# The causal mask as a matrix product, and every fourth low-part subtraction on GpSimd, in a fused decoder block

## The chip, the cores and the metric

One core of a Trainium2 chip runs the whole block in one launch. The metric is the device time of the kernel in microseconds (us); the time of a kernel is the median of its runs. TensorE multiplies matrices, VectorE and ScalarE work elementwise, GpSimd elementwise too and issues the indirect transfers, and SyncE issues most of the others.

## What is computed

Two batches of 1024 tokens of width 256 go through a decoder block in float32: causal self-attention with 16 query heads of 64 and one shared key and value head, cross-attention to 77 context rows, and a feed-forward layer with four experts of which each token takes one. The part that matters here, cut from the reference:

```python
q, k = (l2norm(q), l2norm(k))
q, k = (q * srt, k * srt)            # srt = 4
sim = jnp.einsum('bhid,bjd->bhij', q, k)
causal_mask = jnp.triu(jnp.ones((n, n), dtype=bool), 1)
sim = jnp.where(causal_mask, max_neg, sim)
attn = jax.nn.softmax(sim.astype(jnp.float32), axis=-1)
out = jnp.einsum('bhij,bjd->bhid', attn, v)
```

Since queries and keys have length one before scaling, no score exceeds 16 and the exponentials need no maximum; the row sum comes from a column of ones beside the values.

## The kernel before

**Tiles and steps.** The 2048 tokens are 16 tiles of 128 rows, eight for each batch. The self-attention is a list of 288 steps (t, g, j): tile t, group g of four heads, key tile j from 0 to t mod 8. One step makes a block of scores S, 128 keys by 4 x 128 queries (512 columns), and adds its share to the output O. Tile t has 4 x (t mod 8 + 1) steps; this stretch is called slot t here, and its steps are counted from 0. The last step of each group lies on the diagonal (`on_diagonal`): there keys later than the query must be taken out. There are 64 such steps.

**Precision.** Products in the fast format `F32R` keep fewer bits, so operands are split into a high and a low part. A step takes two products for the scores (L1097, L1098: high and low part of the keys in one tile) and three for the output: values high with `ph` (L1113), values low with `ph` (L1114), values high with `pl` (L1116). `ph` is the exponential rounded to `F32R`, `pr` the exact one, and `pl = pr - ph`.

**Who does what in a step.** TensorE writes S. Off the diagonal ScalarE writes `ph` (L635) and `pr` (L637), and VectorE subtracts (L849). On the diagonal ScalarE writes `pr` only, GpSimd sets the masked part of `pr` to zero (L550), VectorE copies it to `ph` (L847) and then subtracts. `pr`, `ph` and `pl` are rings of four (`RING`); the scores of step k + 3 are issued right after the output products of step k (`AHEAD` = 3).

**Side work.** Between the steps lies all other work of nearby tiles: normalisation, query projection, transposes, output projection, cross-attention, router. `plan_side` spreads it by hand-given positions (`STAGES`), and each engine walks through the same list in `program(engine)`: at position n it does step n and then the side work of position n - `LATER[engine]`. Each engine runs its list in order. GpSimd's side work is mainly powers of -0.5: `roots` of one column (L543), and once per tile the 17 inverse lengths `rn` (L560, stage `qkv_sums`), which waits for VectorE's row sums (L873) and their clamped form `ssc` (L878). After the head outputs are transposed, VectorE scales them (`heads_out`, L900 and L904). Stage `out_proj` ends in a root on GpSimd too.

**After the steps** the tokens are routed, scattered by expert and sent through the experts; the change doesn't touch that.

Of the kernel before, what the change touches and what calls it, by code (L numbers as in the profile page):

```python
# [30 lines left out]
TPB = SEQ // P  # L31
# [3 lines left out]
HPG = HEADS // GROUPS  # L35
# [13 lines left out]
SIM_SCALE = 16.0  # L49
RING = 4  # L50
# [45 lines left out]
AHEAD = 3  # L96


LATER = {"pe": 0, "dve": 2, "act": 3, "pool": 3}
# [85 lines left out]
def build(nc, x, wqkv_t, wout_t, g1, g2, ctx_t, xwq_t, xwk_t, xwv_t, xwout_t, biases, xbout,  # L185
          wr_t, w_v, w_proj, out):
    steps, group_start = plan_steps()
    N_STEPS = len(steps)
# [9 lines left out]
    with ExitStack() as keep:  # L198
        def sem(name):
            return keep.enter_context(nc.semaphore(name))  # L200

        def sb(ctx, name, shape, dt=F32):
            return ctx.enter_context(nc.sbuf_tensor(name, shape, dt))
# [12 lines left out]
        half = sb(keep, "half", [P, HEADS + 2])  # L216
        logits = sb(keep, "logits", [P, TILES, EXP])
# [143 lines left out]
        masked = sem("masked")  # L361
        ph_by_act = sem("ph_by_act")
        ph_by_dve = sem("ph_by_dve")
        pl_ready = sem("pl_ready")
# [71 lines left out]
        def on_diagonal(k):  # L436

            return steps[k][2] == steps[k][0] % TPB

        diagonals = list(itertools.accumulate(int(on_diagonal(k)) for k in range(N_STEPS)))  # L440

        def ph_wait(eng, k):

            if on_diagonal(k):
                eng.wait_ge(ph_by_dve, diagonals[k])
            else:
                eng.wait_ge(ph_by_act, k + 1 - diagonals[k])
# [11 lines left out]
        def _(sp):  # L459
# [19 lines left out]
            sp.wait_ge(consts, 10)  # L479
# [22 lines left out]
        def _(pool):  # L502

            nc.gpsimd.memset(ident[:], 0.0).then_inc(consts, 1)
            nc.gpsimd.memset(tri[:], 1.0).then_inc(consts, 1)
            nc.gpsimd.memset(own[:], 1.0).then_inc(consts, 1)
# [3 lines left out]
            pool.wait_ge(consts, 6)  # L510
# [4 lines left out]
                                    pattern=[[1, P]], channel_multiplier=-1).then_inc(consts, 1)  # L515

# [11 lines left out]
            pool.wait_ge(consts, 10)  # L528
# [16 lines left out]
            for k, stages in program("pool"):  # L545
                if k is not None and steps[k][2] == steps[k][0] % TPB:

                    pool.wait_ge(p_ready, k + 1)
                    blk = pr[:, k % RING, :].rearrange("p (h q) -> p h q", h=HPG)
                    nc.gpsimd.affine_select(out=blk, in_=blk, compare_op=ALU.is_ge, fill=0.0, base=0,  # L550
                                            pattern=[[0, HPG], [1, P]], channel_multiplier=-1).then_inc(masked, 1)
# [59 lines left out]
        def _(act):  # L611
# [14 lines left out]
            for n, (k, stages) in enumerate(program("act")):  # L626
                if k is not None:

                    act.wait_ge(s_ready, k + 1)
                    if k >= RING:  # L630
                        act.wait_ge(pl_ready, k - RING + 1)
                    if not on_diagonal(k):
                        if k >= RING:
                            act.wait_ge(pv_done, k - RING + 1)
                        nc.scalar.activation(ph[:, k % RING, :], S[k % AHEAD][:], ACT.Exp, scale=SIM_SCALE)\  # L635
                            .then_inc(ph_by_act, 1)
                    nc.scalar.activation(pr[:, k % RING, :], S[k % AHEAD][:], ACT.Exp, scale=SIM_SCALE)\  # L637
                        .then_inc(p_ready, 1)
# [122 lines left out]
        def _(dve):  # L761
# [67 lines left out]

            dve.wait_ge(w_in, 32)  # L830
# [3 lines left out]
            diag = 0  # L834
            for k, stages in program("dve"):
                if k is not None:
                    t, _, j = steps[k]

                    if j == t % TPB:
                        diag += 1  # L840
                        dve.wait_ge(masked, diag)
                    else:
                        dve.wait_ge(p_ready, k + 1)
                    if k >= RING:
                        dve.wait_ge(pv_done, k - RING + 1)
                    if on_diagonal(k):
                        nc.vector.tensor_copy(ph[:, k % RING, :], pr[:, k % RING, :]).then_inc(ph_by_dve, 1)  # L847
                    ph_wait(dve, k)
                    nc.vector.tensor_tensor(pl[:, k % RING, :], pr[:, k % RING, :], ph[:, k % RING, :].bitcast(F32),  # L849
                                            ALU.subtract).then_inc(pl_ready, 1)  # L850
# [234 lines left out]
        def _(pe):  # L1085
            pe.wait_ge(consts, 10)
# [12 lines left out]

            def values_of(k):  # L1100
# [256 lines left out]
```

## Time and profile before

| | us |
|---|---|
| median of 3 runs | 1081.1 (1076.33 to 1081.51) |
| the profiled execution, its own time | 1082.78 |
| its span in the profile | 1081.0 |
| TensorE busy | 902.4 |
| VectorE busy | 619.5 |
| ScalarE busy | 545.8 |
| GpSimd busy | 236.9 |

The mean granted clock of TensorE was 0.932 of full speed. Matrix products overlap in the pipeline, so the duration shown for one (about 0.39 us at 512 columns) is longer than the distance between two starts. PE is TensorE, PEld its weight loads, DVE VectorE, ACT ScalarE, POOL GpSimd, SP SyncE.

### The profile page before, as it was taken

The page shows a single profiled execution, that of the slowest core. Times are in us where ns is not written, and L with a number is a line of the kernel's source. Part 1 is how long each engine was busy: PE and PEld are TensorE (multiplying, and loading weights), DVE is VectorE, ACT ScalarE, POOL GpSimd, SP SyncE. Part 2 cuts the span into 40 slices and gives each one's busy share as a digit, 9 for nine tenths or more (in the row PEclk, how much of TensorE's full clock was granted, in tenths as well). Part 3 has the DMA queues.
Part 4 walks back from the last instruction along what each step waited for, and adds up shares of the span by engine and source line. Part 5 has one row for each costly group of instructions (what it writes and reads, how often), then busy time and mean ns, then how long its engine had stood idle before and what let it go on. Part 6 is the DMA issues. An engine that isn't in the chain of part 4 may idle for free.

```text
span 1081.0 us, 14277 instructions
## 1 busy us (share of the span) xinstructions
PE 902.4 (83%) x4446; PEld 672.9 (62%) x4446; DVE 619.5 (57%) x1383; ACT 545.8 (50%) x1032; POOL 236.9 (22%) x282
## 2 busy tenths in 40 slices
PE   3588998989898998969989898999871099999997
PEld 2466676667575765756757575766550077878775
DVE  3456777766666667657676666667576222222221
ACT  1356657566767664455666757676342122222221
POOL 3223322212112122222222222102102501111111
PEclk9688999999999999889999999999975599999999
DMA  8200000000000000000000000000344400000000
GB/s 274 53 1 1 1 2 1 1 1 1 1 1 1 1 1 1 1 1 1 1 1 1 1 1 1 1 1 1 117 139 164 144 11 20 27 21 29 20 25 4
DMA packets 19175, 29.02 MB, mean 27 GB/s; under 512 B 2079, under 2 KB 15648, under 8 KB 19104
## 3 DMA queue, kind: packets, MB, share of 16 engines
q1 hardware_dynamic: 17008, 22.73, 6.9%
q0 software_dynamic: 1680, 4.21, 1.1%
q10 hardware_dynamic: 416, 1.18, 0.3%
q8 instruction: 39, 0.64, 0.2%
q14 instruction: 32, 0.26, 0.1%
HBM read 21.41 MB, written 7.10 MB: 26 GB/s over the span
## 4 chain that ended last, share of the span: by engine, by line
PE 40%; DVE 6%; issue 3%; POOL 3%; ACT 3%; DMA 1%; DVEq 0%; ACTq 0%; POOLq 0%
PE W L1299 7%; PE S L1276 5%; PE O L1276 5%; PE O L1116 2%; PE W L1187 2%; PE S L1097 2%; PE S L1098 2%; PE O L1113 2%; PE O L1114 2%; PE W L1229 2%; POOL sorted_rows L596 2%; PE W L1209 1%; PE W L1155 1%; ACT hT L744 1%; DVE junk L969 1%
## 5 line engine op out<-in xcount | busy, mean ns | idle before, releaser
L849 DVE TENSOR_TENSOR pl<-pr,ph 128x512 fp32r<-128x512 f32 x288 | 199.2, 704 | 48.9 <-ACT pr L637 35.2
L635 ACT ACTIVATE ph<-S 128x512 fp32r<-128x512 f32 x224 | 135.0, 603 | 135.1 <-PE S L1098 133.0
L637 ACT ACTIVATE pr<-S 128x512 f32<-128x512 f32 x288 | 172.3, 600 | 27.9 <-PE S L1098 27.1
L1113 PE MATMUL O<-ph,vhi 128*65 128x512 f32 x288 | 140.8, 489 | 23.7 <-DVE ph L847 23.7
L1116 PE MATMUL O<-pl,vhi 128*65 128x512 f32 x288 | 117.8, 409 | 23.5 <-DVE pl L849 23.1
L1097 PE MATMUL S<-qT,kT 128*128 128x512 f32 x288 | 116.3, 404 | 0.0
L1114 PE MATMUL O<-ph,vlo 128*65 128x512 f32 x288 | 115.6, 401 | 0.0
L1098 PE MATMUL S<-qT,kT 128*128 128x512 f32 x288 | 115.4, 401 | 0.0
L543 POOL TENSOR_TENSOR rs<-ri,half 128x1 f32<-128x1 f32 x48 | 38.9, 811 | 233.5 <-DVE ri L782 233.4
L1116 PEld LDWEIGHTS O<-pl,vhi 128*65 128x65 f32 x288 | 39.9, 138 | 65.5 <-DVE pl L849 40.9
L752 ACT ACTIVATE gate<-S 128x512 f32<-128x512 f32 x38 | 20.7, 596 | 117.7 <-PE S L1276 117.7
L550 POOL TENSOR_SCALAR_AFFINE_SELECT pr<-pr 128x512 f32<-128x512 f32 x64 | 42.6, 666 | 162.9 <-ACT pr L637 162.8
L1299 PE MATMUL W<-wps,hT 128*128 x304 | 70.6, 385 | 8.1 <-ACT hT L744 8.1
L560 POOL TENSOR_TENSOR rn<-ssc,half 128x17 f32<-128x17 f32 x16 | 54.2, 3388 | 102.8 <-DVE ssc L878 102.8
L1155 PE MATMUL W<-wqkv,zT 128*128 128x384 f32 x192 | 72.3, 508 | 0.6 <-ACT zT L647 0.6
L1097 PEld LDWEIGHTS S<-qT,kT 128*128 128x128 f32 x288 | 55.9, 194 | 24.3 <-issue 1.4
L1299 PEld LDWEIGHTS W<-wps,hT 128*128 128x128 f32 x304 | 56.2, 190 | 19.4 <-issue 12.5
L1113 PEld LDWEIGHTS O<-ph,vhi 128*65 128x65 f32 x288 | 40.3, 140 | 39.0 <-DVE ph L847 21.7
L1098 PEld LDWEIGHTS S<-qT,kT 128*128 128x128 f32 x288 | 55.7, 193 | 13.3
L1187 PE MATMUL W<-wout,onT 128*128 128x256 f32 x256 | 60.4, 390 | 1.0 <-DVE xo L950 1.0
L1276 PE MATMUL S<-whl,fzh 128*128 x152 | 56.0, 430 | 2.7 <-DVE fzl L1056 2.7
L425 POOL DMA_INDIRECT out<-res,xs x19 | 19.6, 1031 | 171.8 <-DVE res L1064 171.8
(170 smaller groups left out, 1683.0 us busy)
## 6 DMA issues: line engine op xcount, KB each, us to landing
raw<-in_w_v SPq DMA_DIRECT2D x16, 512.0 KB, 6.3
wps<-in_w_proj SPq DMA_DIRECT2D x4, 1024.0 KB, 8.8
sorted_rows<-pad_row SPq DMA_DIRECT2D x19, 128.5 KB, 4.2
xs<-sorted_rows SPq DMA_DIRECT2D x19, 128.5 KB, 2.0
wqkv<-in_wqkv_t ACTq DMA_DIRECT2D x1, 1152.0 KB, 6.3
wout<-in_wout_t SPq DMA_DIRECT2D x1, 1024.0 KB, 10.0
xall<-in_x SPq DMA_DIRECT2D x1, 1024.0 KB, 10.7
xall<-in_x SPq DMA_DIRECT2D x1, 768.0 KB, 8.0
```

Source lines behind the costliest of these rows:

```text
L635: nc.scalar.activation(ph[:, k % RING, :], S[k % AHEAD][:], ACT.Exp, scale=SIM_SCALE)\
L637: nc.scalar.activation(pr[:, k % RING, :], S[k % AHEAD][:], ACT.Exp, scale=SIM_SCALE)\
L849: nc.vector.tensor_tensor(pl[:, k % RING, :], pr[:, k % RING, :], ph[:, k % RING, :].bitcast(F32), ALU.subtract).then_inc(pl_ready, 1)
L1097: nc.tensor.matmul(S[k % AHEAD][:], kT[:, ks, 0, :], q, start=True, stop=False)
L1098: nc.tensor.matmul(S[k % AHEAD][:], kT[:, ks, 1, :], q, start=False, stop=True).then_inc(s_ready, 1)
L1113: nc.tensor.matmul(o, vhi[:, vs, 0:DH + 1], ph[:, k % RING, :], start=j == 0, stop=False)
L1114: nc.tensor.matmul(o, vlo[:, vs, 0:DH + 1], ph[:, k % RING, :], start=False, stop=False)
L1116: nc.tensor.matmul(o, vhi[:, vs, 0:DH + 1], pl[:, k % RING, :], start=False, stop=last).then_inc(pv_done, 1)
L1155: mm = nc.tensor.matmul(W[job % WB][:, 0:QB], zT[:, c, :], wqkv[:, c, part * QB:(part + 1) * QB], start=c == 0, stop=c == CH - 1)
L1187: mm = nc.tensor.matmul(W[job % WB][:, 0:DIM], onT[:, c, :], wout[:, c, :], start=c == 0, stop=c == 7)
L1276: mm = nc.tensor.matmul(banks[q][:], rows[:, c, :], flat[:, bass.ds(at, 512)], start=m == 0, stop=m == len(passes) - 1)
L1299: mm = nc.tensor.matmul(W[1][:, 0:DIM], hT[:, c, :], flat[:, bass.ds(at, DIM)], start=c == 0, stop=c == HID // P - 1)
```

## The change

The masked positions get -64 added to their score by a product of the identity with a constant block `below` (-64 where the key is later than the query, else 0), accumulated in the same bank ahead of the two score products; with the scale of 16 the exponential of such a score is zero. So ScalarE writes `ph` and `pr` in every step, and GpSimd's select and VectorE's copy are gone. The subtraction of steps k with k mod 4 = 3 runs on GpSimd, the other 216 stay on VectorE. GpSimd's side work comes two positions late in place of three. The setup gets one memset and one select more on GpSimd and two copies on VectorE.

```diff
+MASKED = -64.0
-LATER = {"pe": 0, "dve": 2, "act": 3, "pool": 3}
+LATER = {"pe": 0, "dve": 2, "act": 3, "pool": 2}
...
+        def low_by_pool(k):
+            return k % 4 == 3
+        def low_wait(eng, k):
+            if low_by_pool(k):
+                eng.wait_ge(pl_by_pool, (k + 1) // 4)
             else:
+                eng.wait_ge(pl_by_dve, k + 1 - (k + 1) // 4)
+        def low_part(engine, eng, done, k):
+            eng.wait_ge(p_ready, k + 1)
+            eng.wait_ge(ph_ready, k + 1)
+            if k >= RING:
+                eng.wait_ge(pv_done, k - RING + 1)
+            engine.tensor_tensor(pl[:, k % RING, :], pr[:, k % RING, :], ph[:, k % RING, :].bitcast(F32),
+                                 ALU.subtract).then_inc(done, 1)
...
+            nc.gpsimd.memset(below[:], MASKED).then_inc(consts, 1)
+            nc.gpsimd.affine_select(out=below[:], in_=below[:], compare_op=ALU.is_gt, fill=0.0, base=0,
+                                    pattern=[[-1, P]], channel_multiplier=1).then_inc(consts, 1)
...
             for k, stages in program("pool"):
-                if k is not None and steps[k][2] == steps[k][0] % TPB:
-                    pool.wait_ge(p_ready, k + 1)
-                    blk = pr[:, k % RING, :].rearrange("p (h q) -> p h q", h=HPG)
-                    nc.gpsimd.affine_select(out=blk, in_=blk, compare_op=ALU.is_ge, fill=0.0, base=0,
-                                            pattern=[[0, HPG], [1, P]], channel_multiplier=-1).then_inc(masked, 1)
+                if k is not None and low_by_pool(k):
+                    low_part(nc.gpsimd, pool, pl_by_pool, k)
...
                     act.wait_ge(s_ready, k + 1)
                     if k >= RING:
-                        act.wait_ge(pl_ready, k - RING + 1)
-                    if not on_diagonal(k):
-                        if k >= RING:
-                            act.wait_ge(pv_done, k - RING + 1)
-                        nc.scalar.activation(ph[:, k % RING, :], S[k % AHEAD][:], ACT.Exp, scale=SIM_SCALE)\
-                            .then_inc(ph_by_act, 1)
+                        low_wait(act, k - RING)
+                    if k >= RING:
+                        act.wait_ge(pv_done, k - RING + 1)
+                    nc.scalar.activation(ph[:, k % RING, :], S[k % AHEAD][:], ACT.Exp, scale=SIM_SCALE).then_inc(ph_ready, 1)
                     nc.scalar.activation(pr[:, k % RING, :], S[k % AHEAD][:], ACT.Exp, scale=SIM_SCALE)\
                         .then_inc(p_ready, 1)
...
+            nc.vector.tensor_copy(below_r[:], below[:]).then_inc(mask_ready, 1)
+            nc.vector.tensor_copy(ident_r[:], ident[:]).then_inc(mask_ready, 1)
...
-                    if on_diagonal(k):
-                        nc.vector.tensor_copy(ph[:, k % RING, :], pr[:, k % RING, :]).then_inc(ph_by_dve, 1)
-                    ph_wait(dve, k)
-                    nc.vector.tensor_tensor(pl[:, k % RING, :], pr[:, k % RING, :], ph[:, k % RING, :].bitcast(F32),
-                                            ALU.subtract).then_inc(pl_ready, 1)
+                    if not low_by_pool(k):
+                        low_part(nc.vector, dve, pl_by_dve, k)
...
-                nc.tensor.matmul(S[k % AHEAD][:], kT[:, ks, 0, :], q, start=True, stop=False)
+                if on_diagonal(k):
+                    if k == 0:
+                        pe.wait_ge(mask_ready, 2)
+                    nc.tensor.matmul(S[k % AHEAD][:], ident_r[:], below_r[:].unsqueeze(1).broadcast_to([P, HPG, P]),
+                                     start=True, stop=False)
+                nc.tensor.matmul(S[k % AHEAD][:], kT[:, ks, 0, :], q, start=not on_diagonal(k), stop=False)
                 nc.tensor.matmul(S[k % AHEAD][:], kT[:, ks, 1, :], q, start=False, stop=True).then_inc(s_ready, 1)
...
-                ph_wait(pe, k)
+                pe.wait_ge(ph_ready, k + 1)
...
-                pe.wait_ge(pl_ready, k + 1)
+                low_wait(pe, k)
                 nc.tensor.matmul(o, vhi[:, vs, 0:DH + 1], pl[:, k % RING, :], start=False, stop=last).then_inc(pv_done, 1)
```

## Rows read from the trace of the kernel before

**Rows 1.** The page's first part: busy time of each engine.

```profile
PE 902.4 (83%) x4446; PEld 672.9 (62%) x4446; DVE 619.5 (57%) x1383; ACT 545.8 (50%) x1032; POOL 236.9 (22%) x282
```

**Rows 2.** Stretches: busy us and instructions, granted clock, DMA share, GB/s.

```profile
46.00:768.00 722.00, 645.69 (x3252) 465.86 (x3252) 492.65 (x1058) 458.11 (x878) 167.40 (x196) 0.96 0.00 1
470.60:480.70 10.10, 5.00 (x20) 3.83 (x19) 5.02 (x9) 2.91 (x6) 4.08 (x2) 0.50 0.01 2
```

**Rows 3.** Waits of TensorE, 46 to 768 us: total, times, longest.

```profile
PE O L1113 <- DVE ph L847: 23.7, 12, 6.8
PE O L1116 <- DVE pl L849: 23.1, 19, 3.3
...
PE W L1179 <- DVE on L904: 4.9, 2, 3.8
```

**Rows 4.** Timeline, end of slot 12: start, duration, instruction, idle before.

```profile
602.35 3.48 POOL L560 TENSOR_TENSOR rn<-ssc,half 128x17 f32<-128x17 f32 x1 [7.36 <-DVE ssc L878]
...
607.78 0.63 PE L1116 MATMUL O<-pl,vhi 128*65 128x512 f32 x1
```

**Rows 5.** Timeline, start of slot 10.

```profile
471.61 3.48 POOL L560 TENSOR_TENSOR rn<-ssc,half 128x17 f32<-128x17 f32 x1 [8.44 <-DVE ssc L878]
...
477.00 0.42 DVE L904 TENSOR_TENSOR on<-W,rl 128x256 f32<-128x256 f32 x1
...
477.57 0.66 PE L1217 MATMUL W<-ident,sc 128*128 128x128 f32 x2 [5.10 <-DVE on L904]
```

**Rows 6.** Timeline of a dense stretch of slot 14.

```profile
684.51 0.59 ACT L637 ACTIVATE pr<-S 128x512 f32<-128x512 f32 x1
...
687.03 0.39 PE L1116 MATMUL O<-pl,vhi 128*65 128x512 f32 x1
...
687.26 0.39 PE L1097 MATMUL S<-qT,kT 128*128 128x512 f32 x1
```

**Rows 7.** Groups of instructions: busy us, mean ns; idle before, by whom.

```profile
L849 DVE TENSOR_TENSOR pl<-pr,ph 128x512 fp32r<-128x512 f32 x288 | 199.2, 704 | 48.9 <-ACT pr L637 35.2 <-PE O L1116 8.5 <-DVE logits L969 1.5
...
L635 ACT ACTIVATE ph<-S 128x512 fp32r<-128x512 f32 x224 | 135.0, 603 | 135.1 <-PE S L1098 133.0
...
L550 POOL TENSOR_SCALAR_AFFINE_SELECT pr<-pr 128x512 f32<-128x512 f32 x64 | 42.6, 666 | 162.9 <-ACT pr L637 162.8
...
L847 DVE CAST ph<-pr 128x512 fp32r<-128x512 f32 x64 | 27.7, 432 | 49.1 <-POOL pr L550 48.2 <-PE O L1116 0.7 <-DVE logits L969 0.2
```

**Rows 8.** Single lines on GpSimd: shortest, median, longest ns.

```profile
L576 POOL TENSOR_TENSOR xa<-xa,g2b x16: 724/736/1056, 82.7 to 781.2; 128x256 f32<-128x256 f32 x16
...
L569 POOL CAST vhi<-qhl x16: 237/238/240, 29.3 to 674.8; 128x64 fp32r<-128x64 f32 x16
```

**Rows 9.** Timeline, end of slot 7.

```profile
392.83 3.48 POOL L560 TENSOR_TENSOR rn<-ssc,half 128x17 f32<-128x17 f32 x1 [6.92 <-DVE ssc L878]
...
393.42 0.44 PE L1116 MATMUL O<-pl,vhi 128*65 128x512 f32 x1 [1.28 <-DVE pl L849]
```

**Rows 10.** Timeline, end of slot 3.

```profile
173.46 3.19 POOL L560 TENSOR_TENSOR rn<-ssc,half 128x17 f32<-128x17 f32 x1 [3.33 <-DVE ssc L878]
...
174.68 0.63 PE L1116 MATMUL O<-pl,vhi 128*65 128x512 f32 x1
```

**Rows 11.** Timeline, two products that waited or ran behind a late `pl`.

```profile
512.70 0.45 PE L1116 MATMUL O<-pl,vhi 128*65 128x512 f32 x1
...
708.60 0.45 PE L1116 MATMUL O<-pl,vhi 128*65 128x512 f32 x1 [1.58 <-DVE pl L849]
```

**Rows 12.** Timeline, slot 7: GpSimd's root and a later product.

```profile
361.21 0.96 POOL L543 TENSOR_TENSOR rs<-ri,half 128x1 f32<-128x1 f32 x1 [8.59 <-DVE ri L782]
...
362.63 0.40 PE L1116 MATMUL O<-pl,vhi 128*65 128x512 f32 x1
```

**Rows 13.** Timeline, slot 6: GpSimd and VectorE at once.

```profile
310.26 0.73 POOL L578 TENSOR_TENSOR xall<-xall,xa 128x256 f32<-128x256 f32 x1
310.34 1.20 DVE L849 TENSOR_TENSOR pl<-pr,ph 128x512 fp32r<-128x512 f32 x1
```

More of the change, by code:

```diff
@@ L216, in build @@
         half = sb(keep, "half", [P, HEADS + 2])
+        below = sb(keep, "below", [P, P])
+        below_r = sb(keep, "below_r", [P, P], F32R)
+        ident_r = sb(keep, "ident_r", [P, P], F32R)
         logits = sb(keep, "logits", [P, TILES, EXP])
@@ L360, in build @@
         p_ready = sem("p_ready")
[L361 to L364, printed above, removed]
+        mask_ready = sem("mask_ready")
+        ph_ready = sem("ph_ready")
+        pl_by_pool = sem("pl_by_pool")
+        pl_by_dve = sem("pl_by_dve")
         pv_done = sem("pv_done")
@@ L438, in on_diagonal @@
             return steps[k][2] == steps[k][0] % TPB
-        diagonals = list(itertools.accumulate(int(on_diagonal(k)) for k in range(N_STEPS)))
-        def ph_wait(eng, k):
-            if on_diagonal(k):
-                eng.wait_ge(ph_by_dve, diagonals[k])
-            else:
-                eng.wait_ge(ph_by_act, k + 1 - diagonals[k])
+        def low_by_pool(k):
[3 more added lines that the diff above has]
+                eng.wait_ge(pl_by_pool, (k + 1) // 4)
+            else:
+                eng.wait_ge(pl_by_dve, k + 1 - (k + 1) // 4)
[6 more added lines that the diff above has]
+                                 ALU.subtract).then_inc(done, 1)
         def freed_count(name, part, t):
@@ L477, in _ @@
             sp.wait_ge(x_in[2], 16)
-            sp.wait_ge(consts, 10)
+            sp.wait_ge(consts, 12)
             for n in range(SORTED):
@@ L509, in _ @@
             nc.gpsimd.memset(pad_row[:], 0.0).then_inc(consts, 1)
-            pool.wait_ge(consts, 6)
+            pool.wait_ge(consts, 7)
             nc.gpsimd.affine_select(out=ident[:], in_=ident[:], compare_op=ALU.not_equal, fill=1.0, base=0,
@@ L526, in _ @@
                            channel_multiplier=0).then_inc(consts, 1)
-            pool.wait_ge(consts, 10)
+            pool.wait_ge(consts, 12)
             def roots_of_x(n):
@@ L828, in _ @@
             nc.vector.memset(vlo[:, :, DH:DH + 2].bitcast(F32), 0.0).then_inc(dconst, 1)
+            dve.wait_ge(consts, 12)
+            nc.vector.tensor_copy(below_r[:], below[:]).then_inc(mask_ready, 1)
+            nc.vector.tensor_copy(ident_r[:], ident[:]).then_inc(mask_ready, 1)
             dve.wait_ge(w_in, 32)
@@ L832, in _ @@
                 nc.vector.tensor_scalar(wqkv[:, c, :], wqkv[:, c, :], g1c[:, c:c + 1], None, ALU.mult).then_inc(wq_scaled, 1)
-            diag = 0
             for k, stages in program("dve"):
                 if k is not None:
[L837 to L846, printed above, removed]
-                        nc.vector.tensor_copy(ph[:, k % RING, :], pr[:, k % RING, :]).then_inc(ph_by_dve, 1)
-                    ph_wait(dve, k)
-                    nc.vector.tensor_tensor(pl[:, k % RING, :], pr[:, k % RING, :], ph[:, k % RING, :].bitcast(F32),
-                                            ALU.subtract).then_inc(pl_ready, 1)
+                    if not low_by_pool(k):
+                        low_part(nc.vector, dve, pl_by_dve, k)
                 for name, part, t, job in stages:
@@ L1085, in _ @@
         def _(pe):
-            pe.wait_ge(consts, 10)
+            pe.wait_ge(consts, 12)
             def scores_of(k):
```

## The prediction

> **What bounds the kernel now.** I read the page first. TensorE is busy for 902.4 us of the span of 1081.0 (83%); VectorE follows with 57% [rows 1]. The table of stretches then shows where the change lives. The 288 steps of the causal attention run from 46 to 768 us. There TensorE is busy for 645.7 of 722 us at a granted clock of 0.96, VectorE for 492.7, ScalarE for 458.1 and GpSimd for 167.4 [rows 2]. So about 76 us of that stretch are TensorE's waits, and the rest is its own work. A microsecond added to TensorE's queue costs a microsecond, except where TensorE waits anyway.
>
> Then I asked who makes it wait. Of its waits there, 23.7 us are for the high part `ph` made by VectorE (L847), 23.1 us for the low part `pl` (L849), and two long ones, 3.8 us in slot 2 and 5.1 in slot 10, for the scaled heads (L904) in whose queue a masked block stands [rows 3, 5]. The timeline explains them. Every tile has one GpSimd power of 17 columns, about 3.5 us long, that starts when VectorE has the row sums (`ssc`). GpSimd runs in order, so a mask behind it waits for all of it. In slot 12 the power starts at 602.35 and ends at 605.83; mask, copy and product follow, and the third product of the step starts at 607.78 [rows 4]. In slot 10 the power runs from 471.61 to 475.09; the head scaling, queued on VectorE behind the copy of the masked block, starts at 477.00, and TensorE stands still for 5.1 us, until 477.57 [rows 5].
>
> **The change part by part.** (1) The mask as a product. 64 diagonal steps each get one more 512-column product on TensorE. Products of that width start 0.23 us apart (687.03 to 687.26) [rows 6], so 64 x 0.23 = 14.7 us. At some eleven slot ends TensorE still waits for something else afterwards and the product disappears in that wait: 11 x 0.23 = 2.5. Term: +12.2 us (ends: 6 if half of the 64 are hidden, 15). Its weight load lies under the product before it. The repeated block of `below_r` as moving operand is not in the trace; I take it at the rate of a plain one.
>
> (2) What leaves the diagonal step. GpSimd's select (0.67 us x 64 = 42.6) and VectorE's copy (0.43 x 64 = 27.7) go; ScalarE gets 64 exponentials of 0.60 more [rows 7]. ScalarE has 264 us of idle time in the stretch for 38 us, so I cost these at nothing; they lie under TensorE's products. If that cover were gone, the 38 us would be the price.
>
> (3) The low part of every fourth step on GpSimd. VectorE loses 72 x 0.70 = 51 us. GpSimd's product of two 128x256 operands takes 0.74 us in the median, and its cast of 64 columns 0.24 [rows 8]. Those 192 columns cost 0.50, so 256 more cost at least that: 1.23 at the lower end; twice the 256-column time, 1.47, is the upper. I take 1.35, the middle. In ordinary steps this is hidden. I went through all 72 affected steps for the time from the end of `pr` to the product that reads `pl`. The shortest is 1.93 us: `pr` ends at 685.10, and the product starts at 687.03 [rows 6]. So the GpSimd time has 0.6 us to spare even there.
>
> It isn't hidden behind the power. Every slot has a multiple of four steps, so GpSimd takes local steps 3, 7, 11 and so on. In the step list, with GpSimd's side work now two positions late, the power lands just ahead of such a step in slots of 16 steps (power after step 14, step 15 next: slots 3 and 11) and of 32 (after step 26, step 27 next: slot 7; slot 15 has no power). In slot 7 the power runs from 392.83 to 396.31, and TensorE had `pl` of step 27 at 393.42 [rows 9]. It will have it at 396.31 + 1.35 = 397.7: +4.2. In slot 3: 173.46 + 3.19 + 1.35 = 178.0 against 174.68 [rows 10], +3.3; slot 11, read in the same way, +3.5. Queued behind the waiting product on TensorE are all later scores, and ScalarE's exponentials wait for those, so nothing fills the gap. Term: +11.0 us.
>
> (4) Where the power is followed by a mask today. Slots 4, 5, 6, 12 and 13: the product that read `pl` started 1.85 to 2.04 us after the power's end (1.95 in slot 12 [rows 4]), and will start 1.35 after it, so about 0.6 each: -3.0. Slots 2 and 10: the block of the diagonal step no longer waits for GpSimd, so the head scaling comes right behind VectorE's queue. Slot 10: from 477.57 to about 473.5, -4.1; slot 2 loses its wait of 3.8. Term: -7.9. The first wait, the 6.8 us of [rows 3], ends behind GpSimd's first mask, but VectorE's setup stands ahead of the first step too and GpSimd's power still bounds the next tile's queries: of 0 to 6.8 I take what mask and copy cost by [rows 7] (0.67 + 0.43) and half a us of hand-over: -1.6.
>
> (5) Places where VectorE was late with a step that now is GpSimd's, such as the wait of 1.58 at 708.60 (-1.5) and the product at 512.70, the last step of slot 10, which GpSimd could serve some 1.8 us sooner [rows 11]; five more of about 0.5 each, in slots 6, 7 and 15, are taken for -2.7. Together -6.0. In slots 2, 5, 6, 10 and 13 one moved subtraction lies in VectorE's run up to the row sums, so that the power starts some 0.7 us sooner; about half reaches TensorE: -1.5.
>
> (6) Side work of GpSimd just ahead of its subtraction: the root after the output projection in slot 7 ends at 362.17, so the low part at 363.5, for a product that ran at 362.63 [rows 12]: 0.9 late; slot 15 the same, and a small case of 0.3 in slot 2: +2.1. The two positions in place of three in `LATER` move side work earlier past masks that are gone, and no queue on SP or DMA is touched. The setup's extra memset, select and two copies lie under the weight load that VectorE waits for: 0.
>
> (7) Two engines at one memory port. While GpSimd's addition runs from 310.26 for 0.73 us, VectorE's low part takes 1.20 instead of its mean of 0.70 [rows 7, 13]. So 72 subtractions may hold VectorE 72 x 0.5 = 36 us, less than the 78 us it is freed of. Only what falls into the late runs counts: +1.0 (ends 0 and 16). The Trainium skill ("GPSIMD Engine Reference", Specifications and 4.1 Engine selection) says that GpSimd shares its SBUF interfaces with VectorE, against instructions with two SBUF inputs, and that two-input elementwise work belongs on VectorE. The trace agrees on the sharing, by that 1.20 against 0.70; what it would do to the time is the third rival below.
>
> (8) The clock. After a long wait TensorE runs at half clock for a while: from 470.6 to 480.7 the granted clock is 0.50, the 1.2 GHz level [rows 2]. I take half clock after each new wait for about as long as the wait (3.4 us), which costs half of that, 1.7. The three new waits bring about +5.1; the waits that vanish in slots 2 and 10 give back about 4: +1.1.
>
> **Sum.** Costs 12.2 + 11.0 + 2.1 + 1.0 + 1.1 = 27.4; gains 3.0 + 7.9 + 1.6 + 6.0 + 1.5 = 20.0; net +7.4 us. The profiled execution took 1082.8 us, 1.7 above the median of the runs shown (1081.1). 1082.8 + 7.4 = 1090.2, and at the level of the runs 1088.5, 0.7% slower.
>
> **Rivals.** *The relief of VectorE reaches TensorE (faster).* VectorE loses 51 + 28 = 78 us, 4.9 per slot. If the row sums come 1.5 us earlier in 13 slots and TensorE's waits shrink with them, that is -19.5: 1088.5 - 19.5 = 1069. It decides from 0.6 us per slot on. For it: 23.1 us of waits for `pl`. Against it: the run of VectorE work from the sums of probabilities to `ssc` holds no moved step in most slots. In slot 3 it holds only step 14, and `ssc` comes at 173.4 as before. Chance 0.18.
>
> *The sum cancels.* More products are hidden (6 in place of 12.2) and the idle left after the three new waits is partly won back, because the engines that fed the later waits catch up meanwhile: about 1081. For it: TensorE is idle for 76 us in the stretch, and the terms are differences. Against it: those waits are concentrated at the slot ends, and only one diagonal step in four is there. Chance 0.26.
>
> *GpSimd and VectorE hold each other up (slower still).* Two low parts per slot end on VectorE are each held 0.5 us in 14 slots (+14), and GpSimd's own subtraction takes 0.3 us longer in the eight places where the power precedes it (+2.4): 1088.5 + 16 = 1105. For it: [rows 13]. Against it: the mean of all 288 low parts is 0.70 us [rows 7], so GpSimd's powers and masks, which ran beside many of them, hardly held them. Chance 0.13.
>
> My forecast, within 1083 to 1098 by its own unknowns: chance 0.43.
>
> **Range and chances.** The range reaches from 1076 (part of the faster case) to 1100 (part of the port case). About 0.5%, 5.4 us, is what a measurement of this kernel can tell from no change. The forecast gives faster 0, same 0.06, slower 0.37; the relief faster 0.16, same 0.02; cancelling faster 0.03, same 0.20, slower 0.03; the port case slower 0.13. That is faster 0.19, same 0.28, slower 0.53.
>
> **What would show it.** Right: waits of TensorE on a GpSimd `pl`, some 4 to 5 us long, in slots 3, 7 and 11, right behind the power; no waits for `ph`; no wait over 2 us in slots 2 and 10; GpSimd's subtraction near 1.35 us; 64 products with `ident_r`, 0.23 us apart from their neighbours. Wrong: `ssc` more than 1 us earlier within its slot; a mask product of 0.4 us or more at full clock; GpSimd subtractions of 2 us; or ScalarE as the releaser of long TensorE waits.

## The result, and the profile after

The changed kernel takes 1096.03 us (median of four runs, 1094.67 to 1097.55), the kernel before 1081.12 (four runs on the same chip, 1076.33 to 1081.51). The ratio of all runs is 1.015, with a 95% interval from 1.0124 to 1.0176 (that of the two medians is 1.0138): 14.9 us slower by the medians, where 7.4 were forecast. The direction was right, the size twice the forecast. The profiled execution took 1094.67 us with a span of 1092.7.

The page of the kernel after, first part and two groups of instructions:

```profile
PE 912.7 (84%) x4510; PEld 684.4 (63%) x4510; DVE 568.5 (52%) x1249; ACT 576.4 (53%) x1096; POOL 292.2 (27%) x292
...
L461 DVE TENSOR_TENSOR pl<-pr,ph 128x512 fp32r<-128x512 f32 x216 | 156.9, 734 | 125.9 <-ACT pr L650 112.1
...
L461 POOL TENSOR_TENSOR pl<-pr,ph 128x512 fp32r<-128x512 f32 x72 | 97.4, 1352 | 112.5 <-ACT pr L650 108.9
```

GpSimd gained 55 us against [rows 1], and its subtraction takes the 1.35 us that the sum used. VectorE lost 51 us and not the 78 that the subtractions and copies taken from it had cost. Its own mean low part rose from 704 ns [rows 7] to 734. Now the stretch of the attention steps and one stretch at half clock, columns as in [rows 2]:

```profile
45.00:782.50 737.50, 658.68 (x3311) 480.02 (x3311) 441.32 (x921) 488.23 (x941) 222.73 (x206) 0.96 0.00 1
168.20:178.40 10.20, 5.97 (x21) 4.61 (x22) 3.11 (x6) 3.34 (x7) 5.27 (x3) 0.50 0.00 0
```

The steps take 737.5 us, 14.5 more than before, counted from 45 us to the last step; the rest of the kernel is 2.8 us shorter in these two profiles (spans 1092.7 and 1081.0). TensorE's waits of that stretch, total, times and longest:

```profile
PE O L1125 <- POOL pl L461: 27.5, 12, 5.5
PE O L1125 <- DVE pl L461: 24.5, 17, 3.9
PE W L1180 <- ACT oT L632: 14.9, 21, 2.8
```

The waits for `ph` of [rows 3] are gone, and waits of 27.5 us for GpSimd's `pl` stand in their place; the 23.1 us for VectorE's `pl` did not shrink. The timeline of the end of slot 3, which answers to [rows 10]:

```profile
167.66 3.48 POOL L575 TENSOR_TENSOR rn<-ssc,half 128x17 f32<-128x17 f32 x1 [8.49 <-DVE ssc L882]
171.12 1.26 POOL L461 TENSOR_TENSOR pl<-pr,ph 128x512 fp32r<-128x512 f32 x1
...
172.43 0.69 PE L1125 MATMUL O<-pl,vhi 128*65 128x512 f32 x1 [5.43 <-POOL pl L461]
...
177.14 1.35 DVE L888 TENSOR_TENSOR qn<-qraw,rn 128x1152 f32<-128x1152 f32 x1
177.30 2.33 POOL L461 TENSOR_TENSOR pl<-pr,ph 128x512 fp32r<-128x512 f32 x1 [4.93 <-ACT pr L650]
```

The power ends, the subtraction follows, and TensorE has stood still for 5.43 us; slots 7 and 11 show the same with 5.45 and 5.46. From 168.2, within that wait, to 178.4 the granted clock is half. The last line shows something else: GpSimd's subtraction needs 2.33 us beside a VectorE instruction with two operands. The reverse happens at the end of slot 15:

```profile
770.95 1.39 POOL L461 TENSOR_TENSOR pl<-pr,ph 128x512 fp32r<-128x512 f32 x1 [3.59 <-ACT pr L650]
...
771.24 1.39 DVE L973 CUSTOM_DVE_ANT_0 junk<-z,wrb 128x256 f32<-128x256 f32 x1
...
772.66 0.42 DVE L973 CUSTOM_DVE_ANT_0 junk<-z,wrb 128x256 f32<-128x256 f32 x1
...
774.55 0.45 PE L1125 MATMUL O<-pl,vhi 128*65 128x512 f32 x1 [2.52 <-DVE pl L461]
```

A router product of VectorE takes 1.39 us beside GpSimd and 0.42 without. The next `pl` is late by that 1 us: here TensorE waits 2.52, before the change 1.61. The groups by line tell how often VectorE is held:

```profile
L888 DVE TENSOR_TENSOR qn<-qraw,rn 128x1152 f32<-128x1152 f32 x16 | 31.4, 1963 | 7.1 <-POOL rn L575 7.0
...
L973 DVE CUSTOM_DVE_ANT_0 junk<-z,wrb 128x256 f32<-128x256 f32 x64 | 30.1, 470 | 2.2
...
L1104 PE MATMUL S<-below_r,ident_r 128*128 128x512 f32 x64 | 26.4, 413 | 0.0
```

**A ledger for all that follows.** For the stretch from 45 us to the last attention step I split the length into three: TensorE idle (length less its busy time in the table of stretches), the clock's toll (half of its busy time in the stretches with a granted clock of 0.5), and the rest, which is its work at full clock. These are read from one profiled execution of each kernel, the median is of all its runs. The profiled execution of idle_work_one_input took 1067.3 us, 5 more than its median, that of no_product 1087.8, 5.8 less; the others lie within 2 us.

| kernel | low parts on GpSimd, `LATER` | idle | half clock costs | rest | length | median |
|---|---|---|---|---|---|---|
| before | 0, 3 | 77.3 | 22.4 | 623.2 | 723.0 | 1081.1 |
| after | 72, 2 | 78.8 | 24.8 | 633.9 | 737.5 | 1096.0 |
| mask_only | 0, 2 | 52.7 | 8.6 | 634.7 | 696.0 | 1056.0 |
| mask_only_later3 | 0, 3 | 52.0 | 7.1 | 635.0 | 694.1 | 1054.8 |
| mask_twice | 0, 2 | 51.0 | 5.2 | 648.3 | 704.5 | 1065.1 |
| skip_three | 69, 2 | 67.3 | 16.9 | 635.2 | 719.4 | 1076.7 |
| skip_eight | 64, 2 | 59.2 | 12.9 | 635.0 | 707.1 | 1064.5 |
| later_three | 72, 3 | 66.4 | 20.2 | 633.9 | 720.5 | 1081.2 |
| no_product | 72, 2 | 84.7 | 25.2 | 620.2 | 730.1 | 1093.6 |
| after_logits | 13, 2 | 56.1 | 16.7 | 632.8 | 705.7 | 1063.3 |
| gpsimd_idle_work | 0, 2 | 61.3 | 15.9 | 634.4 | 711.6 | 1067.7 |
| idle_work_one_input | 0, 2 | 56.3 | 16.5 | 634.4 | 707.2 | 1062.3 |
| before_later2 | 0, 2 | 93.2 | 32.3 | 621.9 | 747.4 | 1105.6 |

### The profile page after: what moved, and what is told of

It reads as the page before. It is cut to its first block, busy times and chain, and to the rows that moved or that the text cites. A ratio compares the mean times of both kernels' runs of the same rounds, so it can differ in the third digit from the quotient of the medians.

```text
span 1092.7 us, 14350 instructions
## 1 busy us (share of the span) xinstructions
PE 912.7 (84%) x4510; PEld 684.4 (63%) x4510; DVE 568.5 (52%) x1249; ACT 576.4 (53%) x1096; POOL 292.2 (27%) x292
## 4 chain that ended last, share of the span: by engine, by line
PE 62%; issue 12%; DVE 10%; POOL 8%; ACT 6%; DMA 2%; ACTq 0%; DVEq 0%; POOLq 0%
PE W L1308 6%; PE S L1285 5%; PE O L1285 5%; PE W L1196 5%; PE O L1125 4%; PE S L1107 4%; PE S L1106 4%; PE W L1164 4%; PE O L1122 4%; PE O L1123 4%; POOL rn L575 3%; PE W L1173 3%; PE W L1218 3%; PE W L1238 2%; POOL pl L461 2%
## 5 line engine op out<-in xcount | busy, mean ns | idle before, releaser
L649 ACT ACTIVATE ph<-S 128x512 fp32r<-128x512 f32 x288 | 173.8, 604 | 173.0 <-PE S L1107 170.5
L461 DVE TENSOR_TENSOR pl<-pr,ph 128x512 fp32r<-128x512 f32 x216 | 156.9, 734 | 125.9 <-ACT pr L650 112.1
L1125 PE MATMUL O<-pl,vhi 128*65 128x512 f32 x288 | 118.6, 412 | 52.1 <-POOL pl L461 27.5
L461 POOL TENSOR_TENSOR pl<-pr,ph 128x512 fp32r<-128x512 f32 x72 | 97.4, 1352 | 112.5 <-ACT pr L650 108.9
L1106 PEld LDWEIGHTS S<-qT,kT 128*128 128x128 f32 x288 | 56.3, 195 | 22.6 <-issue 1.1
L1107 PEld LDWEIGHTS S<-qT,kT 128*128 128x128 f32 x288 | 56.1, 195 | 13.5
L1196 PEld LDWEIGHTS W<-wout,onT 128*128 128x128 f32 x256 | 48.6, 195 | 8.6 <-issue 2.3
```

The lines of the kernel that those rows point to most:

```text
L461: engine.tensor_tensor(pl[:, k % RING, :], pr[:, k % RING, :], ph[:, k % RING, :].bitcast(F32), ALU.subtract).then_inc(done, 1)
L1125: nc.tensor.matmul(o, vhi[:, vs, 0:DH + 1], pl[:, k % RING, :], start=False, stop=last).then_inc(pv_done, 1)
L1196: mm = nc.tensor.matmul(W[job % WB][:, 0:DIM], onT[:, c, :], wout[:, c, :], start=c == 0, stop=c == 7)
```

## Experiments

Ratios are to the kernel before, run on the same chip, with the 95% interval.

**mask_only: the mask as a product, all low parts on VectorE.**

```diff
         def low_by_pool(k):
-            return k % 4 == 3
+            return False
```

Here and below, the counts that the waits for `pl` use are taken from a running sum of the steps on GpSimd.

> The mask as a product stays; all 288 low parts are subtracted by VectorE and none by GpSimd. Theory A (the loss is GpSimd's low parts that stand behind its power of 17 columns; the product itself is paid for by the waits for `ph` that vanish): 1070 to 1080 us, not slower than the kernel before, and no wait of TensorE over 3.5 us on a low part. Theory B (the 64 products on TensorE are the loss, and moving the subtractions changes nothing): 1090 to 1097 us.

1055.95 us, ratio 0.9775 [0.9748, 0.9802]: theory B is refuted, and theory A's range was 14 us too high. One half of the change alone makes the kernel 25 us faster, so the other half costs 40 (with two positions in `LATER`; later_three splits it). The stretch and the waits of TensorE in it:

```profile
45.00:741.00 696.00, 643.34 (x3311) 470.14 (x3309) 462.30 (x993) 487.68 (x941) 131.99 (x133) 0.99 0.00 1
```

```profile
PE O L1127 <- DVE pl L463: 25.6, 20, 3.9
PE W L1182 <- ACT oT L634: 14.2, 24, 1.7
```

Against [rows 2] the granted clock is 0.99 in place of 0.96. The 23.7 us of waits for `ph` [rows 3] vanished; those for `pl` rose by 2.5 us and those for `oT`, ScalarE's copy of the head outputs, from 11.0 to 14.2. The ledger: products +11.5, idle -24.6, half clock -13.8.

**skip_three: the three subtractions behind the power back on VectorE.** They are steps 39, 139 and 183, in slots 3, 7 and 11.

```diff
-            return k % 4 == 3
+            return k % 4 == 3 and k not in (39, 139, 183)
```

> The changed kernel, but the three low parts right behind the power (the last step of slots 3 and 11 and step 27 of slot 7) go back to VectorE; 69 stay on GpSimd. Theory A in its narrow form (these three are the main loss): 1080 to 1086 us. Rival A2 (the loss lies in all slots where a GpSimd low part comes within a few steps behind the power, or in VectorE and GpSimd holding each other up): 1088 to 1093 us. Theory B: 1093 to 1097 us.

1076.73 us, ratio 0.9975 [0.9954, 0.9996], 3 us under the range of theory A: three subtractions of 72 cost 19.3 us (each interval alone is some 2 to 3 us wide on either side). The ledger gives the parts: 11.5 of waits, 7.9 of half clock.

**skip_eight: those three and the five of slots 4, 5, 6, 12 and 13**, which also run right behind the power.

```diff
-            return k % 4 == 3
+            return k % 4 == 3 and k not in (39, 59, 83, 111, 139, 183, 203, 227)
```

> As skip_three, but all eight low parts that come next behind the power (one in each of slots 3, 4, 5, 6, 7, 11, 12 and 13) go back to VectorE; 64 stay on GpSimd. mask_only took 1056 us and skip_three 1077. Theory W (what is left is mostly TensorE waiting for GpSimd low parts behind the power, 11 us in skip_three, and the half clock after them): 1060 to 1066 us. Theory C (what is left is mostly VectorE held up while GpSimd reads two operands, which 64 low parts still do): 1070 to 1076 us.

1064.49 us, ratio 0.9871 [0.9847, 0.9895], in the range of theory W: 12.2 less than skip_three, though none of the five waits is longer than 2.8 us in the kernel after; 8.1 of it are waits, 4.0 half clock. Of the waits for GpSimd's `pl` 2.0 us are left, none over 0.7:

```profile
PE O L1127 <- DVE pl L463: 28.3, 20, 3.9
...
PE O L1127 <- POOL pl L463: 2.0, 4, 0.7
```

The other 64 subtractions are hardly waited for and still cost 8.5 us (1064.5 against 1056.0), so theory C has its share too.

**later_three: the changed kernel with GpSimd's side work three positions late, as before.**

```diff
-LATER = {"pe": 0, "dve": 2, "act": 3, "pool": 2}
+LATER = {"pe": 0, "dve": 2, "act": 3, "pool": 3}
```

> The changed kernel with GpSimd's side work three positions late in place of two, as it was before; the same 72 low parts on GpSimd. In slots 3, 7 and 11 the power now comes right behind the moved step and not ahead of it, so theory A expects what skip_three gives, 1080 to 1086 us, without moving a single subtraction. Rival: the later roots cost as much as is won, 1094 us or more.

1081.2 us, ratio 1.001 [0.9994, 1.0026], in the range of theory A: one number of the change is worth 14.8 us. The end of slot 3 in the timeline, and the waits:

```profile
163.98 1.26 POOL L461 TENSOR_TENSOR pl<-pr,ph 128x512 fp32r<-128x512 f32 x1 [5.50 <-ACT pr L650]
...
167.90 3.48 POOL L575 TENSOR_TENSOR rn<-ssc,half 128x17 f32<-128x17 f32 x1 [2.65 <-DVE ssc L882]
```

```profile
PE O L1125 <- DVE pl L461: 28.6, 17, 4.0
...
PE O L1125 <- POOL pl L461: 10.1, 6, 2.8
```

One position later the low part of step 15 runs ahead of the power and not behind it; the 27.5 us of waits for GpSimd's `pl` become 10.1.

**before_later2: the kernel before with two positions in place of three, nothing else.**

```diff
-LATER = {"pe": 0, "dve": 2, "act": 3, "pool": 3}
+LATER = {"pe": 0, "dve": 2, "act": 3, "pool": 2}
```

> The kernel before with GpSimd's side work two positions late in place of three, and nothing else of the change. There the power meets masks: in slots 5 and 6 and from 9 on it then comes ahead of other diagonal steps than before. If the number in LATER is a free choice, within 4 us of the kernel before; if it is worth something by itself, over 1085 or under 1077 us.

1105.58 us, ratio 1.0224 [1.0199, 1.0248], 24 us slower: the number is no free choice. The timeline at the end of slot 3 shows the same collision with the mask in the subtraction's place:

```profile
175.10 3.08 POOL L560 TENSOR_TENSOR rn<-ssc,half 128x17 f32<-128x17 f32 x1 [7.71 <-DVE ssc L878]
178.15 0.63 POOL L550 TENSOR_SCALAR_AFFINE_SELECT pr<-pr 128x512 f32<-128x512 f32 x1
178.82 0.43 DVE L847 CAST ph<-pr 128x512 fp32r<-128x512 f32 x1 [3.79 <-POOL pr L550]
...
179.30 0.69 PE L1113 MATMUL O<-ph,vhi 128*65 128x512 f32 x1 [5.34 <-DVE ph L847]
```

**mask_only_later3: mask_only with three positions.** The edits of mask_only and of later_three together.

```diff
+LATER = {"pe": 0, "dve": 2, "act": 3, "pool": 3}
...
+            return False
```

> mask_only with GpSimd's side work three positions late, as before, in place of two. GpSimd waits for no step at all in mask_only, so only the order of its side work against itself could matter: 1054 to 1058 us, the same as mask_only within 2 us. If over 1060 us or under 1052, the number in LATER has a weight of its own that the prediction left out.

1054.76 us, ratio 0.9756 [0.9731, 0.9781], as expected, and not to be told from mask_only. Where no step waits for GpSimd, the position of its side work is worth nothing here. It is the fastest kernel here, 26 us under the one before and 41 under the changed one.

**no_product: the changed kernel without the mask product.** It leaves the mask out, so every query sees all keys of its diagonal tile.

```diff
-                if on_diagonal(k):
...
-                    nc.tensor.matmul(S[k % AHEAD][:], ident_r[:], below_r[:].unsqueeze(1).broadcast_to([P, HPG, P]),
-                                     start=True, stop=False)
-                nc.tensor.matmul(S[k % AHEAD][:], kT[:, ks, 0, :], q, start=not on_diagonal(k), stop=False)
+                nc.tensor.matmul(S[k % AHEAD][:], kT[:, ks, 0, :], q, start=True, stop=False)
```

> The changed kernel without the 64 mask products: nothing is masked on the diagonal, so the output lacks the causal mask inside the diagonal blocks; all else is as in the changed kernel. The step of the prediction (52 of 64 products exposed at 0.23 us) expects 12.2 us less than the changed kernel, 1084 us. If most products hide in waits: 1089 to 1092 us. If they cost more than their 0.23 us, by a slower read of the repeated block or by the clock: 1078 us or less.

1093.57 us (1087.78 to 1096.33), ratio 1.0122 [1.0089, 1.0155]. The median is 2.5 us below the changed kernel and not the 12.2 that the term of the prediction expects, and it lies above all three ranges. The runs scatter by 8.5 us, and the profiled one, whose span is 6.9 us shorter, is the fastest of the six. So the products are not what makes the kernel slow. In that execution the ledger has 13.7 us less work, of which 5.9 turned into waits.

**mask_twice: mask_only with each mask product issued twice** (the masked scores get -128).

```diff
                     nc.tensor.matmul(S[k % AHEAD][:], ident_r[:], below_r[:].unsqueeze(1).broadcast_to([P, HPG, P]),
                                      start=True, stop=False)
+                    nc.tensor.matmul(S[k % AHEAD][:], ident_r[:], below_r[:].unsqueeze(1).broadcast_to([P, HPG, P]),
+                                     start=False, stop=False)
```

> mask_only with the mask product issued twice in each of the 64 diagonal steps, so that 64 products more are accumulated (the masked scores get -128 instead of -64). If a product costs what the prediction's first step says (0.23 us each, four in five exposed): 1067 to 1071 us. If the half of them or more hides in waits: 1063 us or less. If the repeated block or the clock makes it dearer: over 1072 us.

1065.05 us, ratio 0.9867 [0.9846, 0.9887], between two of the ranges: +9.1 for 64 more products. Their work is 13.6 us, or 0.21 each, in the ledger; 5.1 come back from waits and from the clock. In the timeline such products start 0.23 apart:

```profile
209.08 0.39 PE L1106 MATMUL S<-below_r,ident_r 128*128 128x512 f32 x1
...
209.31 0.39 PE L1108 MATMUL S<-below_r,ident_r 128*128 128x512 f32 x1
```

**gpsimd_idle_work: mask_only, and GpSimd does 72 subtractions of the same shape that nobody waits for**, on constant operands, at every fourth step. Like the low part, each waits until `pr` of its step is there (the diff leaves out the waits).

```diff
-                if k is not None and low_by_pool(k):
-                    low_part(nc.gpsimd, pool, pl_by_pool, k)
+                if k is not None and k % 4 == 3:
...
+                    nc.gpsimd.tensor_tensor(wk[:].rearrange("p c n -> p (c n)"), wout[:, 0:2, :].rearrange("p c n -> p (c n)"),
+                                            wout[:, 2:4, :].rearrange("p c n -> p (c n)"), ALU.subtract).then_inc(idle_sem, 1)
```

> mask_only (all low parts on VectorE) plus a subtraction of the same size and form on GpSimd in each of the 72 steps, on other buffers (two halves of the output projection's weights, into a buffer that is no longer used), for which no engine waits. It adds only GpSimd's time and its reading of two operands. Theory C: 1064 us or more, VectorE's mean low part clearly over 0.70 us. Theory W: 1056 to 1060 us.

1067.73 us, ratio 0.9878 [0.9853, 0.9903], as theory C has it: 11.8 us for work that feeds nothing, while VectorE has all 288 low parts. The groups by line:

```profile
L464 DVE TENSOR_TENSOR pl<-pr,ph 128x512 fp32r<-128x512 f32 x288 | 217.5, 765 | 72.3 <-ACT pr L661 61.7 <-PE O L1136 6.7 <-DVE logits L984 2.2
L576 POOL TENSOR_TENSOR wk<-wout 128x512 f32<-128x512 f32 x72 | 109.7, 1524 | 82.1 <-ACT pr L661 66.4 <-issue 8.3 <-DVE on L919 4.2
L899 DVE TENSOR_TENSOR qn<-qraw,rn 128x1152 f32<-128x1152 f32 x16 | 32.5, 2032 | 6.3 <-POOL rn L586 6.1
```

VectorE's low part is at 765 ns against 699 in mask_only, the scaling of the queries at 2032 against 1354. VectorE does the same work in both kernels, and is busy for 626.2 us against 590.2: 36 us, or 0.5 for each of the 72 subtractions.

**idle_work_one_input: as gpsimd_idle_work, with two copies in place of the subtraction**, each of one operand.

```diff
-                    nc.gpsimd.tensor_tensor(wk[:].rearrange("p c n -> p (c n)"), wout[:, 0:2, :].rearrange("p c n -> p (c n)"),
-                                            wout[:, 2:4, :].rearrange("p c n -> p (c n)"), ALU.subtract).then_inc(idle_sem, 1)
+                    nc.gpsimd.tensor_copy(wk[:].rearrange("p c n -> p (c n)"), wout[:, 0:2, :].rearrange("p c n -> p (c n)"))\
+                        .then_inc(idle_sem, 1)
+                    nc.gpsimd.tensor_copy(wv[:].rearrange("p c n -> p (c n)"), wout[:, 2:4, :].rearrange("p c n -> p (c n)"))\
+                        .then_inc(idle_sem, 1)
```

> As gpsimd_idle_work (1068 us against 1056 of mask_only), but in place of the one subtraction of two 512-column operands GpSimd makes two copies of 512 columns, each with one operand, so that it is busy about as long (some 0.65 us each by the select of that size in the kernel before). Theory C in its sharp form (what hurts is that GpSimd reads two operands while VectorE wants two as well): 1056 to 1060 us. Rival Q (what hurts is GpSimd's queue: its power and roots come later): 1064 to 1069 us.

1062.31 us (1059.61 to 1069.46), ratio 0.9832 [0.9801, 0.9864]: 6.4 us over mask_only, between the two ranges, with wide scatter. VectorE is held here too, about half as much:

```profile
L464 DVE TENSOR_TENSOR pl<-pr,ph 128x512 fp32r<-128x512 f32 x288 | 209.3, 735 | 81.4 <-ACT pr L663 71.1 <-PE O L1138 6.9 <-DVE logits L986 2.0
L578 POOL COPY wv<-wout 128x512 f32<-128x512 f32 x72 | 67.7, 941 | 0.0
L576 POOL COPY wk<-wout 128x512 f32<-128x512 f32 x72 | 59.9, 832 | 82.7 <-ACT pr L663 71.0 <-issue 8.2 <-DVE sc L950 2.9
...
L588 POOL TENSOR_TENSOR rn<-ssc,half 128x17 f32<-128x17 f32 x16 | 55.3, 3459 | 112.9 <-DVE ssc L895 112.9
```

The last row speaks against rival Q: GpSimd idled ahead of the powers until `ssc` came. In the traces of this kernel, of gpsimd_idle_work and of mask_only each of the 16 powers and 48 roots of one column starts within 0.1 us of the end of the VectorE instruction that it needs, so none of them was held up in GpSimd's queue.

**after_logits: only 13 low parts on GpSimd**, those that in mask_only stand behind a run of VectorE work (mostly the router's products) and make TensorE wait.

```diff
-            return k % 4 == 3
+            return k in (38, 57, 80, 107, 138, 148, 156, 167, 182, 201, 224, 251, 282)
```

> mask_only, but 13 chosen low parts go to GpSimd: in each slot from 3 on the one that VectorE reaches only behind its four router products, where TensorE waits 1.0 to 3.0 us for VectorE; all of them are ahead of the power. Theory W (a low part in front of which GpSimd is free relieves VectorE): 1045 to 1052 us. Theory C (while GpSimd subtracts, VectorE's router products, which read two operands, stand still, so the wait moves to the next step): 1054 to 1060 us.

1063.29 us, ratio 0.9855 [0.9834, 0.9877], 7.3 us over mask_only and 3 over the range of theory C; the ledger has 3.4 more of idle time and 8.1 of half clock. Even in the places chosen for it, the help of GpSimd is a loss:

```profile
PE O L1127 <- DVE pl L463: 26.4, 14, 3.9
```

The waits for `pl` are fewer (14 in place of 20) and together as long (26.4 us against 25.6). Most moved to a neighbouring step: in slot 3 waits of 0.9 and 1.3 us became one of 2.6. The router's products take 518 ns on average, against 425 in mask_only.

## Why the prediction was wrong in size

The sum of +7.4 was made of three kinds of term. The ledger of before and after has +14.5 for the stretch.

| | forecast | ledger |
|---|---|---|
| mask products at full clock (14.7, less what hides) | +14.7 | +10.7 |
| TensorE's idle time | -8.4 | +1.5 |
| clock | +1.1 | +2.4 |

(Forecast idle: 11.0 + 2.1 + 1.0 of costs less 20.0 of gains and the 2.5 of hidden products.) So the idle time is where the sum failed, by 9.9 us, partly covered by products that came 4 us cheaper in this ledger. The steps that failed are (5), the relief of VectorE, and the last part of (7), how much of its holding reaches TensorE. The runs show that behind the net lie larger errors of opposite sign.

**Term (1), the mask products: right in the work, uncertain in what shows.** They start 0.23 us apart, repeated operand and all. 64 more in mask_twice add 13.6 us of work and 9.1 to the time, where the term was 12.2 (ends 6 and 15). Taking the 64 out of the changed kernel gives 2.5 back, with a scatter of 8.5 (no_product), so there more of them may lie in other waits than at the eleven slot ends that the term counted.

**Term (2), ScalarE's 64 further exponentials at nothing: nearly right.** TensorE's waits for ScalarE's `oT` rose from 11.0 us to 14.9, the longest from 2.0 to 2.8, and to 14.2 in mask_only. No run shows whether the exponentials are the cause.

**Steps (2) and (4), what the removed select and copy were worth: too small.** The prediction priced the two against GpSimd's subtraction that would stand in their place: 0.6 us each in five slots, 7.9 in slots 2 and 10, 1.6 at the start. The amounts for slots 2 and 10 and for the start were about right: the wait of 5.1 us in slot 10 [rows 5] is gone, and that slot is 5.7 us shorter (forecast 4.1), slot 2 by 2.7 (forecast 3.8).

The sign "no wait over 2 us in slots 2 and 10" failed all the same: slot 2 has one of 2.2 us for `oT`, slot 10 one of 3.0 for `pl`. In slots 4, 5, 6, 12 and 13 the waits at the block behind the power were 10.8 us in all and are 9.2 now, where 3.0 less were forecast.

But with nothing on GpSimd in their place the mask as a product saves 24.6 us of waits and 13.8 of clock, shown by mask_only. The prediction never priced the two halves of the change apart, and so did not see that one of them is good: 25 us faster.

**Step (3), three subtractions behind the power: right in place, wait and mechanism.** Forecast were waits of 4 to 5 us in slots 3, 7 and 11, worth 11.0; the trace has 5.4 to 5.5 three times, and skip_three gives 11.5 for them. With the clock they come to 19.3 (forecast 11.0 + 5.1 = 16.1).

**Step (5), the relief of VectorE: failed.** It was to give 6.0 + 1.5 us, and the runs show none. TensorE's waits for VectorE's `pl` went from 23.1 to 24.5 us although a quarter of the low parts had left. The wait of 1.58 at 708.60 [rows 11], forecast to vanish, shows why. The kernel after at the same place in slot 14:

```profile
714.84 1.28 POOL L461 TENSOR_TENSOR pl<-pr,ph 128x512 fp32r<-128x512 f32 x1 [0.46 <-ACT pr L650]
...
715.11 1.56 DVE L461 TENSOR_TENSOR pl<-pr,ph 128x512 fp32r<-128x512 f32 x1
...
716.72 0.45 PE L1125 MATMUL O<-pl,vhi 128*65 128x512 f32 x1 [0.51 <-DVE pl L461]
...
720.37 0.45 PE L1125 MATMUL O<-pl,vhi 128*65 128x512 f32 x1 [1.14 <-DVE pl L461]
```

The moved step itself no longer waits. But GpSimd's subtraction for it holds VectorE's low part of the step before (1.56 us), and the step behind it waits for the same router products: 0.51 + 1.14 in place of 1.58. `ssc` came no sooner either. Measured from the last output product of the slot before, the powers of slots 5, 6 and 13, which were to start 0.7 us sooner, start 2.0, 1.0 and 1.3 us later. One at the start of slot 3 comes 1.3 us sooner, but it does so in mask_only too, where no subtraction moved.

In slot 10 of the kernel before, TensorE's last product ahead of the power waited for VectorE and started 2.05 us ahead of it (the power is at 471.61 [rows 5]):

```profile
469.56 0.45 PE L1116 MATMUL O<-pl,vhi 128*65 128x512 f32 x1 [3.25 <-DVE pl L849]
```

The same place in the timeline of the kernel after:

```profile
479.43 0.69 PE L1125 MATMUL O<-pl,vhi 128*65 128x512 f32 x1 [3.01 <-DVE pl L461]
...
481.48 3.49 POOL L575 TENSOR_TENSOR rn<-ssc,half 128x17 f32<-128x17 f32 x1 [7.96 <-DVE ssc L882]
...
484.94 1.28 POOL L461 TENSOR_TENSOR pl<-pr,ph 128x512 fp32r<-128x512 f32 x1
...
485.00 2.43 DVE L888 TENSOR_TENSOR qn<-qraw,rn 128x1152 f32<-128x1152 f32 x1 [1.80 <-POOL rn L575]
```

The distance is 2.05 us again, and behind the power GpSimd's low part slows VectorE's scaling of the queries to 2.43 us. after_logits shows that the 13 steps chosen for it don't bring the relief.

**Step (7), the shared port: right in the holding, far too small in what reaches TensorE.** The step had 72 x 0.5 = 36 us of holding, and gpsimd_idle_work measures 36. But it took only +1.0 of them as falling into late runs (ends 0 and 16). Work of GpSimd that nobody waits for costs 11.8 us (gpsimd_idle_work), the 64 nearly harmless subtractions of skip_eight 8.5. Against mask_only the changed kernel takes 72 x 0.70 = 50 us of subtractions from VectorE, and its busy time falls by 21.7 (590.2 to 568.5); the other 29 came back as holding, where the relief of step (5) should have been. The mechanism is the one that [rows 13] showed. The third rival had it at +16 with a chance of 0.13, and the truth lies between.

What that rival had against itself was the mean of VectorE's low part, 0.70 us [rows 7], beside GpSimd's powers and masks. Powers indeed hold nothing: in the trace before, 32 low parts overlap one of 17 columns and take 0.69 us, as alone. Selects do: four query scalings that overlap one take 1.78 us in place of 1.35, which that mean can't show. The Trainium skill ("GPSIMD Engine Reference", 4.1 Engine selection) advises VectorE for elementwise work, because GpSimd is about twice as slow with two inputs. The trace agrees, with 1352 ns against 734 for the same subtraction; the runs add a price of 8.5 to 11.8 us for 64 to 72 of them. idle_work_one_input costs 6.4 us, so about half of the price came without a second operand on GpSimd.

**Step (6), `LATER`: priced in step (3), but taken for a given.** Step (3) saw that with two positions the power lands ahead of step 15, and its 16.1 us with the clock are this number's price: later_three has 14.8. What the text missed is that the low parts don't need the number. With three positions the three waits of step (3) don't exist. In the kernel before two positions cost 24 us (before_later2), in mask_only nothing.

**Step (8), the clock: right in kind, small amounts.** Half clock comes with the three new waits, as forecast, for 6.8 to 10.2 us each, and costs 7.1 for them where the step had 5.1. But it was counted for these waits only. mask_only gains 13.8 us from it, and the low parts on GpSimd cost 16.2 (8.6 to 24.8): over half a us of clock for each us of idle time, 13.8 for 24.6 and 16.2 for 26.1. It is no fixed rate: after_logits loses 8.1 for 3.4.

**The whole, by runs:** mask as a product at three positions -26.3 (1081.1 to 1054.8), 72 low parts on GpSimd +26.4 (1081.2 in later_three), two positions in place of three +14.8: 1096.0. That the forecast of 1088.5 came within 8 us was luck: two errors of more than 20 us, in the gain of the mask and in the cost of the low parts, nearly cancelled. The rival of relief is refuted. That of cancelling is too; its 1081 is what later_three takes, but there by the mask's gain against the low parts' cost.

**What stays open:** which of the held instructions make TensorE wait. VectorE is held 36 us in gpsimd_idle_work and the kernel is 11.8 slower; the ledger splits this into 8.6 of idle time and 7.3 of half clock, not by instruction. GpSimd's queue can't be it by way of powers and roots, which start as promptly as in mask_only; what little other side work stands behind the idle work (4 and 8 instructions in the two kernels) wasn't tested. The step ledger can't say why 64 products are 10.7 us in one pair of kernels and 13.6 in another; a few matmul records may be missing.

## What to carry to other kernels

Price the two halves of a change apart, each against the kernel before, also where they meet in one place; a net of small terms hides a good half and a bad one. Before giving an in-order engine work that others wait for, find its longest instruction and look what stands right behind it: one position decides 15 to 24 us here. Work taken from VectorE by GpSimd isn't gone for VectorE (29 of 50 us came back here); try it with idle work of the same shape first.

## What the hardware showed that I had not expected

- The holding is nearly a full exclusion and goes both ways; in these cases the one that started first kept its time. VectorE's router product took 1.39 us in place of 0.42 beside GpSimd's subtraction; the subtraction took 2.33 in place of 1.26 beside VectorE's scaling of the queries. That scaling went from a mean of 1354 ns (mask_only) to 1963.
- One-operand copies on GpSimd (832 and 941 ns at 512 columns) hold VectorE too: in idle_work_one_input its low part rose from 699 to 735 ns, against 765 beside the subtractions.
- GpSimd's powers don't hold it: 32 low parts of VectorE beside one took 0.69 us, as alone.
- Waits under 3 us can cost clock as well. In the kernel after, those of 2.8 us in slots 4 and 12 come with 6.8 and 3.4 us at half clock; around those of 1.7 and 1.6 in slots 5 and 13 the granted clock is 1.00. With most long waits gone (mask_only), the mean granted clock of the stretch rose from 0.96 to 0.99.
